# Scores: the low part of k against 64 rows of q, on both halves of the array

## What is computed

```
q, k, v = split(x @ w_qkv.T + b_qkv)            # 8 batch rows, 8 heads, 512 x 64 each
scores  = einsum('bhfc,bhtc->bhft', k, q)        # f: key position, t: query position
scores  = where(f <= t, scores, -10000)
attn    = softmax(scores, axis=f)
vals    = einsum('bhft,bhfc->bhtc', attn, v)
```

## Time and profile before

| | |
|---|---|
| median of 3 runs | 1414.14 us (1413.69 to 1414.88) |
| profiled execution | 1414.13 us, its span 1412.3 us |
| TensorE products | 7796, busy 1396.6 us (99%) |
| TensorE weight loads | 7796, busy 1247.1 us (88%) |
| VectorE, GpSimdE, ScalarE | busy 1046.3, 704.1, 692.8 us |
| score products (L1554) | 512, from 38.6 to 810.7 us |

### The profile page before, as it was taken

The page is one execution under the profiler, slowest core; times in us unless marked ns, Lnnn a source line. Parts: engine busy times, 40 slices in busy tenths (PEclk is TensorE's granted clock), DMA queues, the critical chain, the costliest instruction groups (busy, mean ns, idle before and its releaser), DMA issues.

```text
span 1412.3 us, 25002 instructions
## 1 busy us (share of the span) xinstructions
PE 1396.6 (99%) x7796; PEld 1247.1 (88%) x7796; DVE 1046.3 (74%) x2204; ACT 692.8 (49%) x1498; POOL 704.1 (50%) x1268
## 2 busy tenths in 40 slices
PE   7999999999999999999999999999999999999998
PEld 6888888888888888888888889999999999999997
DVE  7676685776775776766756888898878787878764
ACT  6365465564573664654654764433333333333332
POOL 3364462571562553644624775555555555555542
PEclk9999999999999999999999999999999999999999
DMA  7434334324433343343333643322222222222311
GB/s 253 142 127 120 143 104 154 134 95 138 145 111 123 126 137 138 115 127 138 112 99 94 213 139 116 104 107 98 96 92 101 104 104 91 90 94 96 119 75 60
DMA packets 71797, 168.55 MB, mean 119 GB/s; under 512 B 7760, under 2 KB 31568, under 8 KB 71760
## 3 DMA queue, kind: packets, MB, share of 16 engines
q1 hardware_dynamic: 71760, 168.09, 35.3%
HBM read 62.15 MB, written 25.69 MB: 62 GB/s over the span
## 4 chain that ended last, share of the span: by engine, by line
PE 91%; issue 3%; POOL 2%; DVE 1%; POOLq 1%; ACT 1%; DMA 1%; DVEq 1%; SPq 0%; ACTq 0%
PE ps_f L2471 23%; PE ps_o L1503 21%; PE ps_o L1534 12%; PE ps_s L1554 6%; PE ps_o L2356 6%; PE ps_v L1370 6%; PE ps_t L1408 3%; PE ps_o L1497 3%; PE ps_z L2356 2%; PE ps_f L2417 2%; PE ps_o L1573 2%; PE ps_x L2407 1%; PE ps_v L1378 1%; PE ps_t L1503 1%; PE ps_o L1454 1%
## 5 line engine op out<-in xcount | busy, mean ns | idle before, releaser
L2471 PE MATMUL ps_f<-wagh,x2Th 128*128 128x364 f32 x756 | 250.9, 332 | 0.0
L2471 PE MATMUL ps_f<-wagh,x2Tl 128*128 128x364 f32 x756 | 248.7, 329 | 0.0
L2471 PE MATMUL ps_f<-wagl,x2Th 128*128 128x364 f32 x756 | 248.3, 329 | 0.0
L1503 PE MATMUL ps_o<-xTh,wh 128*128 128x512 f32 x424 | 172.3, 406 | 0.0
L1503 PE MATMUL ps_o<-xTh,wl 128*128 128x512 f32 x424 | 166.5, 393 | 0.0
L1503 PE MATMUL ps_o<-xTl,wh 128*128 128x512 f32 x424 | 165.7, 391 | 0.0
L583 POOL TENSOR_SCALAR pr<-pr,nwm,rden 128x512 f32<-128x512 f32 (+3 forms) x256 | 159.7, 638 | 11.3 <-issue 11.3
L559 POOL TENSOR_TENSOR cw<-wm,cnt 128x4 f32<-128x4 f32 x64 | 12.8, 200 | 300.3 <-ACT pr L1134 300.3
L2471 PEld LDWEIGHTS ps_f<-wagh,x2Th 128*128 128x128 f32 x756 | 142.0, 188 | 2.2 <-issue 0.3
L2471 PEld LDWEIGHTS ps_f<-wagl,x2Th 128*128 128x128 f32 x756 | 142.3, 188 | 1.5
L2471 PEld LDWEIGHTS ps_f<-wagh,x2Tl 128*128 128x128 f32 x756 | 142.3, 188 | 0.0
(11 more groups left out here) (309 smaller groups left out, 3438.3 us busy)
## 6 DMA issues: line engine op xcount, KB each, us to landing
p_words<-pr SPq DMA_DIRECT2D x56, 448.0 KB, 2.8
kst<-kst SPq DMA_DIRECT2D x64, 256.0 KB, 3.7
x<-in_x SPq DMA_DIRECT2D x31, 512.0 KB, 3.9
x2r<-x2n SPq DMA_DIRECT2D x30, 512.0 KB, 2.9
xs<-in_x SPq DMA_DIRECT2D x24, 512.0 KB, 4.6
out<-x SPq DMA_DIRECT2D x23, 512.0 KB, 2.7
p_words<-pr SPq DMA_DIRECT2D x56, 192.0 KB, 2.3
xs_words<-xs SPq DMA_DIRECT2D x21, 512.0 KB, 3.2
```

Of the source, the lines that this page charges most:

```text
L1503: done = pe.matmul(ps[:, :], w[:, k, c:c + P], xT[:, k, :], start=(k == 0 and w is wh and xT is xTh), stop=(k == KD - 1 and w is wl), skip ...
L2471: last = pe.matmul(ps_f[:, g, 0:GW], a[:, k, :], w[:, k, cols], start=(k == 0 and a is xh and w is wagh), stop=False, skip_group_check=True)
```

## The change

The four products with k's high part stay as they are and come first, in the order of blocks 3, 2, 0, 1. The four with k's low part then take only the 64 rows with q's high part: blocks 2, 1 and 0 on the head's own half of the array, block 3 on the other half. There q's high part of block 3 is needed in the other 64 rows, so ScalarE copies these 128 columns into a new tile `q_copy` behind each `q_hi` (after a wait for its own q_high), and TensorE waits for `q_copied`. The product of the two low parts is no longer computed. To make room `pr` is laid into the bytes of `p_words`, so that the move of `pr` to `p_words` reads and writes the same place.

```diff
+        q_copy = sb("q_copy", [P, 2, P], F32R)
+        ones = sb("ones", [P, 2], F32R)
+        with ExitStack() as early:
+            pr = sb("pr", [P, 2, PT_N], F32, early)
         p_words = sb("p_words", [P, 2, PT_N], F32R)
-        ones = sb("ones", [P, 2], F32R)
-        pr = sb("pr", [P, 2, PT_N], F32)
...
                 last.then_inc(q_high, 1)
+                act.wait_ge(q_high, 4 * b + p + 1)
+                for s in range(2):
+                    own, other = (slice(0, HD), slice(HD, P)) if s == 0 else (slice(HD, P), slice(0, HD))
+                    last = act.activation(q_copy[other, p % 2, :], qst[p % 2][own, s, 3 * P:4 * P].bitcast(F32), ACT.Copy)
+                last.then_inc(q_copied, 1)
...
                     pe.wait_ge(q_low, 4 * b + p + 1)
+                    pe.wait_ge(q_copied, 4 * b + p + 1)
...
-                for i in range(NT):
-                    for part in range(2):
-                        last = pe.matmul(ps_s[:, PS_OFF[i]:PS_OFF[i] + (i + 1) * P],
-                                         qst[p % 2][:, s, i * P:(i + 1) * P],
-                                         kst[p % 2][:, s, part, 0:(i + 1) * P],
-                                         start=(part == 0), stop=(part == 1), skip_group_check=True)
+                own, other = (slice(0, HD), slice(HD, P)) if s == 0 else (slice(HD, P), slice(0, HD))
+                for i in (3, 2, 0, 1):
+                    pe.matmul(ps_s[:, PS_OFF[i]:PS_OFF[i] + (i + 1) * P], qst[p % 2][:, s, i * P:(i + 1) * P],
+                              kst[p % 2][:, s, 0, 0:(i + 1) * P], start=(i != 1), stop=False, skip_group_check=True)
+                for i, rows in ((3, other), (2, own), (1, own), (0, own)):
+                    q_rows = q_copy[other, p % 2, :] if i == 3 else qst[p % 2][own, s, i * P:(i + 1) * P]
+                    last = pe.matmul(ps_s[:, PS_OFF[i]:PS_OFF[i] + (i + 1) * P], q_rows,
+                                     kst[p % 2][rows, s, 1, 0:(i + 1) * P], start=False, stop=True, skip_group_check=True)
```

More of the change, by code:

```diff
@@ L255, in attention_phase @@
         ve_done = sem("ve_done")
+        q_copied = sem("q_copied")
         words_landed = [sem(f"words_landed{i}") for i in range(3)]
```

## The result

The changed kernel takes 1421.86 us (median of 4 runs, 1421.52 to 1423.56), the kernel before 1414.43 us beside it (1413.69 to 1414.88): ratio 1.0055, 95% interval 1.004 to 1.007. The change makes the kernel slower by 7.4 us. The forecast was 1406; the range (1396 to 1430) holds the time, with rival 2's sign at half of rival 2's size.

What follows compares the result with a forecast made beforehand. The kernel was taken as bound by the rate at which TensorE takes products in. Score groups -18.0, passages +5.1, ScalarE's delays +1.0 and +3.5 sum to -8.4 us from 1414.13: 1406 us, range 1396 to 1430.

Steps and rivals of the forecast that it cites:

- rival 2: Each TensorE switch between whole and half array empties it: 0.247 us, twice a group, 31.6 us; 1429 us, chance 0.33.
- narrow products between wide ones: Score groups on TensorE: the new order hides the 128-wide product's load, 0.095 us a group, 6.1 us less.
- two halves side by side: The 512-wide half product runs beside the three narrower ones: 0.418 us a group instead of 0.605; 12.0 us less.
- 128 passages: TensorE going from whole array to half or back, twice in each of 64 groups: 0.04 us each, 5.1 us more.
- copies and what they delay: ScalarE's added copies make work behind them late for TensorE in pairs 2 and 3: 4.5 us more.
- The four whole ones: The four whole-array score products, one of each width, cost half a value group of L1370: 1.21 / 2 = 0.605 us.
- Pair 2: Head 4's scores wait for the copy back of L1076, 0.1 to 0.2 us late in 7 loop turns: 1.0 us.
- pair 3: Copies delay head 5's exponentials, and through head 6 the move of p and TensorE's transposes: 0.5 us in 7 turns, 3.5 us.
- q_copied at nothing: TensorE's added wait for ScalarE's copy costs nothing: it shares an instruction and the copy is ready long before its scores.
- 1: The halves don't run together; only the order's 6.1 us is gained: about 1415 us, chance 0.12.
- 3: Weights of the same half can't load under a running product: 24.2 us more, 1430 us, chance 0.04.
- 4: The chain through ScalarE makes pairs 2 and 3 late by 8.4 us: 1410 us; chance 0.51 together with the forecast.

Runs made afterwards that it cites:

- e1: The changed kernel with all eight score products on the whole array in the new order, no copies, no q_copied: 1412.65 us, 0.9991 of the kernel before.
- e3: The changed kernel without its two copies per pair; block 3's half product takes the 64 rows as they are: 1418.29 us, 1.0027 of the kernel before.
- e4: As e3, but all four half products on the head's own half, one behind the other: 1432.84 us, 1.0131 of the kernel before.
- e6: As e1, but each group's last product (256 columns, k's low part) on the head's own half: 1432.68 us, 1.0144 of the kernel before.
- e9: The kernel before with only its score blocks reordered to 3, 1, 2, 0, whole array: 1413.01 us, 0.9994 of the kernel before.
- e2: As e1, plus the change's two ScalarE copies a pair and TensorE's wait for q_copied: 1416.77 us, 1.0021 of the kernel before.
- e7: The changed kernel with ScalarE's copies of pairs 2, 3 and the next row's pair 0 moved behind steps others wait for: 1423.95 us, 1.0071 of the kernel before.
- e5: As e3, but each score group goes to the half array and back twice: 1446.12 us, 1.0229 of the kernel before.

## Why the prediction was wrong

**The ledger**, by the prediction's own terms. The passages and the side by side are taken from e1, e3, e4 and e6:

| term | predicted us | measured us |
|---|---|---|
| narrow products between wide ones | -6.1 | -1.3 (e1), -0.9 (e9) |
| two halves side by side | -12.0 | -14.6 (e3 less e4) |
| 128 passages | +5.1 | +20.0 to +20.2 (e6, e4 less e1) |
| copies and what they delay | +4.5 | +4.1 (e2 less e1), +3.1 to +4.0 (change less e3) |
| sum | -8.4 | +7.2 to +8.4, against 7.4 measured |

- *What bounds the kernel*: right. Every edit of a group arrived at the end nearly whole: 64 x 0.227 = 14.5 against 14.6 us.
- *The four whole ones, "half of what a value group holds"*: **wrong**. The 1.21 us of a value group is not its whole cost; a narrow product leaves about 0.05 us to its successor, outside of the group. e9 reached 1.21 us in the scores and lost it behind them. Of the 6.1 us that this step was worth, 1.3 at most are there.
- *The half ones, "the second product starts behind the first by 0 to 80 ns; I take 40"*: nearly right, they start together, and the gain is 14.6 us instead of 12.0.
- *"I take half of the nearest row, 0.04 us" for a passage*: **wrong, the step that turned the sign**. It is 0.158 us, four times that and above the 0.141 from which rival 2 was to decide. (That bound leaves out the sum's own 4.5 us of waits; with them the gain is gone at (18.0 - 4.5) / 128 = 0.105 us.) The reason I gave, that a load could be issued ahead for another part of the array, is what the trace denies: at a passage the load starts with its product, and the first half products are 0.10 us longer than their like. The mechanism of rival 2 (results come out, then the first load shows) fits what the rows show; its price, 0.247 us from adding the two rows, was half as much too high. The timelines of e4 say where: the wait for the results is 0.09 us and not the 0.167 of an empty array, while the load shows with 0.05 to 0.10 us, near the 0.08 taken for it.
- *ScalarE's copies, 1.0 + 3.5 us*: the size was near (3.1 to 4.1), the chain too. Pair 2 cost some 0.6 us (0.08 a turn, e3 to the change), not 1.0. The wait of pair 3 came mostly at head 7's scores (0.27 us a turn), less at head 6's transposes (0.11).
- *q_copied at nothing*: in the change, yes; in e7 waits of 0.33 and 0.30 us came up as soon as the copies stood later.
- *Rivals*: 1 and 3 fell with e4 and e6. 4 did not occur as such; its waits did, but nearer to the 4.5 us of the sum than to its own 8.4. With only the order's term corrected the forecast would have been some 1411, still a gain; the passages, 15 us above their term, turn it into a loss.

The Trainium skill, "TensorEngine Tiling (Array Packing)", section "Key Properties", has it that a change of the tiling mode drains the engine, and a change of the tile within the mode does not. The runs agree with both: 0.158 us a passage in e4 and e6, and in e3, where the widest is on one half and the next on the other, the second starts 0.003 us behind the first. The emptying is not a whole one by these rows: the next load starts 0.08 us before the modelled end of the last product. I had its rule before me and left it out of the sum because no row showed it. It was a rule against the change with a trigger that the diff plainly pulls 128 times, and it deserved more than 0.33.

**No version beats both kernels** by more than the runs can tell: the best, e1_whole and e9_order, are at 0.9991 and 0.9994 of the kernel before.

## What to carry to other kernels

A product on part of the rows saves time only if what runs beside it in one stay is worth more than going there and back: here 0.315 us of TensorE against the 0.227 us of the 512 columns that ran beside the others, so gather more partial products into a stay, or stay on the whole array. And price a product by the time of its group together with its successors: a narrow product's cost shows in the one behind it, and an order that only moves it past the edge of the group gains nothing.

## What the runs showed of the hardware that I had not expected

- Passing between products on all 128 rows and products on 64 rows costs 0.158 us each way on average at a granted clock of 2.4 GHz (e4 and e6, 128 passages; 0.174 us with 256 in e5), with one half product between as with four. The load behind a passage starts with its product instead of 0.12 us ahead, and the product 0.07 instead of 0.16 us before the end of the one in front.
- Two products on different halves start within 0.01 us of each other and run fully beside each other: 14.6 us for 64 products of 512 columns.
- A product behind a 128-wide one on the whole array lasts about 0.05 us longer than its like elsewhere (333 against 279 ns for 256 columns, e1 and e9); the time of a group that ends with a narrow product leaves this out.
